# A mixture-of-experts block after cross attention: another order of routing, and low rank tables in one comparison

## The chip, the cores and the metric

The kernel runs on one core of a Trainium2 chip. The metric is the device time in microseconds of one execution.

## The reference, cut to what matters

`x` and a context are 4 batches of 256 tokens with 256 features. `x` is normalised, attends to the context with 16 heads of 16 features under a causal mask (keys and values are the context itself), and is added to the result. The sum is normalised again and goes through 16 experts, of which each token takes the best four:

```python
logits = x @ router_weight.T + router_bias
top_val, top_idx = jax.lax.top_k(logits, 4)
top_val = softmax(top_val)
gate_up = einsum('th,ehd->etd', x, gate_up_proj) + gate_up_proj_bias
glu = gate * sigmoid(gate * 1.702)          # gate and up clipped at 7
out = einsum('etd,edh->eth', (up + 1.0) * glu, down_proj) + down_proj_bias
x = x + (out * router_scores).sum(over experts)
```

## The kernel before, in words

The 1024 tokens are 8 tiles of 128, two per batch. There is no scheduler: each engine has one list of instructions in the order in which the code issues it, with semaphores between the engines. The list `steps` (built by `slot(b)`, once per batch) gives the order of the units of attention to all engines at once: "T" transposes queries and keys, "X" and "M" find row maxima, "S" is a pair of score matmuls (then the exponential on ScalarE and the causal select on POOL), "V" weighs the values, "O" turns a batch's output for VectorE. In the slot of the last batch the list also carries pieces of the routing of earlier batches: "Y" turns normalised tokens of a batch (TensorE), with a high part copied by ScalarE (`tokens_high`) and a low part by VectorE (`tokens_low`); "L" is the router's logits; "R" the ranks of each token among those of its expert. Routing goes by parts, not batches: part 0 is the first two batches (4 tiles), part 1 the third batch, part 2 the fourth (2 tiles each). `late` names the pieces that are issued by hand behind the list.

Per part, in this order:

- `router_logits` (TensorE, L1334, hi and lo part of the tokens, four matmuls a tile), then `router_logit` and `router_top` (VectorE, L966 to L993): logits, best four, their index, a one-hot `mask` of the experts chosen.
- `router_scores` (VectorE, L1003 to L1009): the softmax over the four, written beside the tokens into `y_ext`. The SyncE queue (SP) sends tokens and scores to DRAM, `y_rows(part)`, L467. `top_exp` on ScalarE gives it the exponential.
- `ranks` (TensorE, L1346, L1350) and `places` (VectorE, L1022 to L1033): from the mask a rank per (token, choice), split into the row inside a block of 128 (`low_f`) and a block number (`vblk_f`).
- For each of the 32 pairs of a tile and a choice two tables of 128 x 128 in f16: `low_hot` (`hot_lows`, VectorE, L1041, one tensor_scalar a pair) and `vblk_hot` (`hot_blocks`, POOL, L595, or `hot_highs`, VectorE, L1048). Part 0 has 16 pairs, parts 1 and 2 have 8 each.
- `slots` (TensorE, L1376): 32 matmuls over these pairs in one sum.

`counted` on POOL (L588) repeats the mask for `counts` (TensorE, L1360), from which `live_blocks`, `places` on TensorE (L1367) and `picks` find the 47 live blocks of tokens. `block_slots` (L1385, L1388) and `slot_tokens` (L1071 to L1075) give the token of each row. Then POOL gathers each block's tokens from DRAM by index (L646; the first six ahead of the loop, and only when all `y_rows` are in DRAM, which is `y_out`), and 47 expert blocks run: L1467 turns the tokens, L1489 is gate and up, L1508 down, L653 adds the rows back.

`rsqrt(b, which)` on POOL (L521) is the power instruction between a batch's variance and `tokens(b)` (VectorE, L849), which normalises it. For the last batch `attn_out`, `x1_rows`, `variance` (L892 to L845) stand ahead of it. `scores_t` (L1428) and `down_rows` (L1440) prepare the bias of the down projection; for parts 1 and 2 they stand behind `block_slots`, ahead of the first expert block.

Around the change VectorE, POOL, ScalarE and TensorE each have a tail written by hand behind the loop over `steps`.

## Time and profile before

| what | us |
|---|---|
| median of 3 runs | 312.12 (310.56 to 316.17) |
| profiled execution, own time | 311.56 |
| its span on the core | 309.8 |
| TensorE busy | 270.8 (87%) |
| POOL busy | 194.1 (63%) |
| VectorE busy | 182.3 (59%) |
| ScalarE busy | 122.8 (40%) |

The span runs from the first to the last instruction of the core; 1.76 us of the execution's own time lie outside it. Attention ends at about 103 us of the span, the expert blocks run from about 133 us to the end, and the routing lies between, partly inside attention's last slot. A busy share says little in that middle stretch: it is the waits that are to be read.

### The profile page before, as it was taken

To read this page: it belongs to the slowest core of one execution; us is meant where nothing else is said; L and a number is where in the kernel's file an instruction comes from. 1 tells how busy PE (TensorE), PEld (TensorE's weight loads), DVE (VectorE), ACT (ScalarE), POOL (GpSimd) and SP (SyncE) were. 2 spreads that over 40 slices of the span, in tenths; PEclk is the share of its full clock that TensorE was granted. 3 is DMA by queue.
4 is the path that set the end of the run, shared out by engine and by line. 5 is a ranking of instruction groups with operands and counts; after the bars stand their busy time and mean duration, and the time that the engine had idled before them with its cause. 6 is when DMAs were issued, how large, how long until landed. Compare 5 with 4: busy or idle time off the path is not lost.

```text
span 309.8 us, 5709 instructions
## 1 busy us (share of the span) xinstructions
PE 270.8 (87%) x1548; PEld 182.6 (59%) x1566; DVE 182.3 (59%) x505; ACT 122.8 (40%) x289; POOL 194.1 (63%) x239
## 2 busy tenths in 40 slices
PE   7787897897989743799998998999999999999895
PEld 7665475465565532555565665666566665656484
DVE  3997748957877978115444554455445466556433
ACT  3426555355464210143443443444434444434410
POOL 5983726524435889541876776877877877776400
PEclk9999998999997855569999999999999999999999
DMA  7706210100369872074554465445445545445464
GB/s 243 236 3 203 70 54 0 43 14 0 102 212 347 269 268 72 19 212 152 78 90 81 70 87 91 70 73 87 89 72 82 93 74 89 86 71 76 105 213 135
DMA packets 26877, 34.33 MB, mean 111 GB/s; under 512 B 2800, under 2 KB 21200, under 8 KB 26848
## 3 DMA queue, kind: packets, MB, share of 16 engines
q0 software_dynamic: 8592, 12.32, 24.6%
q1 hardware_dynamic: 17984, 21.39, 21.1%
q8 instruction: 15, 0.25, 0.3%
q10 hardware_dynamic: 272, 0.26, 0.2%
q14 instruction: 14, 0.11, 0.1%
HBM read 23.46 MB, written 10.43 MB: 109 GB/s over the span
## 4 chain that ended last, share of the span: by engine, by line
PE 62%; DVE 12%; POOL 9%; issue 6%; DMA 5%; ACT 2%; SPq 1%; another core or an unknown queue 1%; ACTq 0%; DVEq 0%
PE ps L1489 24%; PE ps L1508 10%; POOL vblk_hot L595 7%; DVE neg_max L872 6%; PE ps L1227 4%; PE ps L1522 3%; PE ps L1467 3%; DMA ctx_tok<-y_rows,slot_tok 3%; PE ps L1303 3%; PE ps L1498 3%; PE ps L1485 2%; PE ps L1246 2%; PE ps L1279 2%; DMA br_sb<-n_L_ffn_router_bias_dram 2%; PE ps L1440 1%
## 5 line engine op out<-in xcount | busy, mean ns | idle before, releaser
L1489 PE MATMUL ps<-w_all,q_norm 128*128 x188 | 89.6, 599 | 3.4 <-issue 1.9
L653 POOL DMA_INDIRECT acc_rows<-x_tok,slot_tok x44 | 70.0, 1591 | 32.6 <-ACT x_tok L808 27.2
L1151 DVE TENSOR_SCALAR v_aug<-ps 128x256 f32<-128x256 f32 x47 | 20.0, 425 | 72.3 <-PE ps L1489 46.2
L646 POOL DMA_INDIRECT ctx_tok<-y_rows,slot_tok x47 | 46.5, 989 | 16.7 <-issue 14.0
L1508 PEld LDWEIGHTS ps<-w_all,o_t 128*128 128x128 f32 x188 | 35.6, 190 | 25.7 <-issue 23.2
L792 ACT ACTIVATE v_aug<-v_aug 128x256 f32<-128x256 f32 x47 | 19.6, 417 | 76.9 <-DVE v_aug L1151 76.9
L1489 PEld LDWEIGHTS ps<-w_all,q_norm 128*128 128x128 f32 x188 | 35.2, 192 | 24.9 <-issue 23.2
L1508 PE MATMUL ps<-w_all,o_t 128*128 x188 | 48.3, 380 | 1.4 <-ACT o_t L797 1.4
L557 POOL TENSOR_SCALAR_AFFINE_SELECT w_all<-w_all 128x256 f32<-128x256 f32 (+1 forms) x48 | 23.3, 502 | 38.0 <-ACT w_all L706 37.1
L872 DVE TENSOR_REDUCE neg_max<-ps 128x2 f32<-128x512 f32 (+1 forms) x48 | 30.5, 684 | 7.4 <-PE ps L1252 5.1
L706 ACT ACTIVATE w_all<-ps 128x512 f32<-128x512 f32 x48 | 25.5, 601 | 23.3 <-PE ps L1279 23.1
L808 ACT ACTIVATE x_tok<-ps,ctx_tok 128x256 f32<-128x256 f32 x47 | 22.3, 474 | 19.8 <-PE ps L1508 18.9
L595 POOL TENSOR_SCALAR vblk_hot<-iota_h,vblk_f,tok_id 128x128 f16<-128x128 f16 x28 | 22.8, 826 | 2.3 <-DVE vblk_f L1031 2.3
L1162 DVE TENSOR_TENSOR v_aug<-v_aug 128x256 f32<-128x256 f32 x47 | 20.0, 426 | 7.1 <-ACT v_aug L792 5.5
L1169 DVE SCALAR_TENSOR_TENSOR o_t<-v_aug 128x256 f32<-128x256 f32 x47 | 20.0, 426 | 4.6 <-DVE v_aug L1162 0.4
L1467 PE MATMUL ps<-ident,ctx_tok 128*128 128x128 f32 x94 | 18.6, 282 | 1.4 <-DMA ctx_tok<-y_rows,slot_tok 1.3
L1156 DVE TENSOR_SCALAR v_aug<-ps 128x256 f32<-128x256 f32 x47 | 19.5, 415 | 0.0
L1246 PE MATMUL ps<-k_t,q_t 64*128 64x256 f32 (+1 forms) x128 | 13.6, 310 | 6.2 <-DVE neg_max L872 3.5
L786 ACT ACTIVATE q_norm<-ps 128x256 f32<-128x256 f32 x47 | 18.1, 384 | 0.3 <-PE ps L1467 0.3
L1498 PE MATMUL ps<-ident,o_t 128*128 128x128 f32 x94 | 18.0, 273 | 0.0
L1303 PE MATMUL ps<-w_all,v_aug 128*32 128x256 f32 x128 | 16.8, 409 | 1.0 <-ACT o_t L714 0.6
L797 ACT ACTIVATE o_t<-ps 128x256 f32<-128x256 f32 x47 | 17.6, 375 | 0.0
(155 smaller groups left out, 382.3 us busy)
## 6 DMA issues: line engine op xcount, KB each, us to landing
w_all<-_L_ffn_gate_up_proj_dram SPq DMA_DIRECT2D x16, 512.0 KB, 5.2
w_all<-in_L_ffn_down_proj_dram SPq DMA_DIRECT2D x16, 256.0 KB, 5.8
acc_rows<-x_tok SPq DMA_DIRECT2D x8, 256.0 KB, 9.1
x_tok<-in_x_dram SPq DMA_DIRECT2D x4, 256.0 KB, 4.4
y_ext<-acc_rows SPq DMA_DIRECT2D x4, 256.0 KB, 3.6
vblk_hot<-acc_rows SPq DMA_DIRECT2D x4, 256.0 KB, 3.7
out_dram<-y_ext SPq DMA_DIRECT2D x4, 256.0 KB, 2.2
ctx_tok<-in_ctx_dram SPq DMA_DIRECT2D x3, 256.0 KB, 5.1
```

The source lines that it names most:

```text
L557: pool.affine_select(out=blk, in_=blk, compare_op=ALU.is_ge, fill=0.0, base=0, pattern=[[0, n], [1, P]], channel_multiplier=-1).then_inc(s ...
L595: pool.tensor_scalar(vblk_hot[:, j, :], iota_h[:, :], vblk_f[:, j:j + 1], tok_id[:, j // TOP_K:j // TOP_K + 1], ALU.is_equal, ALU.mult).th ...
L646: pool.indirect_dma_start(out=xg[:, i % XG, :], out_offset=None, in_=y_dram[:, :], in_offset=bass.IndirectOffsetOnAxis(ap=slot_tok[:, i:i ...
L653: pool.indirect_dma_start(out=acc[i % 2][:, :], out_offset=bass.IndirectOffsetOnAxis(ap=slot_tok[:, i:i + 1], axis=0), in_=o_sb[:, i % 3, ...
L706: act.activation(prob[:, u % P_RING, :], ps[:, u % ST_RING, :], ACT.Exp, scale=SC).then_inc(exp_done, 1)
L808: act.activation(o_sb[:, i % 3, :], ps[:, 6 + i % 2, 0:D], ACT.Copy, scale=xg[:, i % XG, bass.ds(e + D, 1)]).then_inc(o_ready, 1)
L872: dve.tensor_reduce(neg_max[:, b % 2, t, p0 // 4, s, p0 % 4:p0 % 4 + np_], ps[:, work_bank(u), :].rearrange("p (a k) -> p a k", k=keys), A ...
L1303: pe.matmul(ps[rows, PVB, col:col + S], v_aug[:, b % 2, 0, h, :], p0, start=True, stop=True, skip_group_check=True)
L1467: tr = pe.transpose(ps[:, 2 + i % 2, k * P:(k + 1) * P], xg[:, i % XG, k * P:(k + 1) * P], ident[:, :])
L1489: mm = pe.matmul(o, x_t[:, i % 3, k, :], w_all[:, bass.ds(e, 1), k * 2 * F:(k + 1) * 2 * F].rearrange("p a n -> p (a n)"), start=False, st ...
L1498: tr = pe.transpose(ps[:, 4 + i % 2, f * P:(f + 1) * P], hid[:, i % 2, f * P:(f + 1) * P], ident[:, :])
L1508: mm = pe.matmul(o, hid_t[:, i % 2, f, :], w_all[:, bass.ds(e, 1), at:at + D].rearrange("p a n -> p (a n)"), start=(f == 0), stop=(f == FD ...
```

## The change

The third batch (part 1) gets its logits and ranks inside the last slot, where before only part 0 had them. In `slot`, for the last batch (Y, L and R take a batch or a part):

```diff
-                         ("V", b, (0,)), ("S", b, (5,)), ("V", b, (1, 2, 3)), ("R", 0, (0,)), ("V", b, (4,)),
-                         ("Y", 2, (0,)), ("V", b, (5, 6, 7)), ("O", b, (0, 1))]
+                         ("V", b, (0,)), ("Y", 2, (0,)), ("S", b, (5,)), ("V", b, (1, 2)), ("R", 0, (0,)),
+                         ("V", b, (3,)), ("L", 1, (0,)), ("V", b, (4, 5, 6, 7)), ("R", 1, (0,)), ("O", b, (0, 1))]
...
-        late = [("L", 1, 0), ("Y", B - 1, 0), ("R", 1, 0), ("L", 2, 0), ("R", 2, 0)]
+        late = [("Y", B - 1, 0), ("L", 2, 0), ("R", 2, 0)]
```

On POOL the power instruction of the third batch stands behind S1 of the last slot instead of S4, and the tables of part 1 are no longer POOL's:

```diff
-                    if n == 4 and b >= 1:
+                    if n == (1 if b == B - 1 else 4) and b >= 1:
                         rsqrt(b - 1, 1)
...
             counted(0)
-            hot_blocks(0, pairs_of(0)[:8])
+            hot_blocks(0, pairs_of(0)[:4])
+            counted(1)
+            hot_blocks(0, pairs_of(0)[4:8])
             rsqrt(B - 1, 1)
-            counted(1)
             hot_blocks(0, pairs_of(0)[8:])
-            hot_blocks(1, pairs_of(1))
             counted(2)
             hot_blocks(2, pairs_of(2)[:4])
```

On VectorE the low tables of a part are one comparison of two broadcast operands, and the order is another:

```diff
-                for j in pairs_of(part):
-                    ins = dve.tensor_scalar(low_hot[:, j, :], iota_h[:, :], low_f[:, j:j + 1], None, ALU.is_equal)
-                ins.then_inc(low_hot_ready, 1)
+                pairs = pairs_of(part)
+                n = len(pairs)
+                dve.tensor_tensor(low_hot[:, pairs.start:pairs.stop, :], iota_h[:, :].unsqueeze(1).to_broadcast([P, n, P]),
+                                  low_f[:, pairs.start:pairs.stop].unsqueeze(2).to_broadcast([P, n, P]), ALU.is_equal
+                                  ).then_inc(low_hot_ready, 1)
...
                 elif kind == "L":
                     router_logit(b)
+                    if b == 0:
+                        tokens(B - 2)
                     router_top(b)
-                    router_scores(b)
+                    if b == 1:
+                        router_scores(0)
                 elif kind == "R":
                     places(b)
-                    hot_lows(b)
-
-            router_logit(1)
+
+            router_scores(1)
             tokens(B - 1)
-            router_top(1)
+            hot_lows(0)
             tokens_low(B - 1)
-            places(1)
+            hot_highs(1, pairs_of(1))
+            hot_lows(1)
             router_logit(2)
             router_top(2)
-            router_scores(1)
-            router_scores(2)
             places(2)
-            hot_lows(1)
             hot_lows(2)
             hot_highs(2, pairs_of(2)[4:])
             live_blocks()
+            router_scores(2)
             picks()
```

On ScalarE `top_exp(1)` comes first behind the loop. On TensorE the tail is:

```diff
-            router_logits(1)
             scores_t(0)
             down_rows(0)
+            tokens_t(B - 1)
             down_rows(1)
-            tokens_t(B - 1)
-            ranks(1)
             router_logits(2)
-            slots(0)
             ranks(2)
             counts()
+            slots(0)
+            slots(1)
             places()
-            slots(1)
             slots(2)
```

Beside this, `neg_half` becomes a view of a tile `small` that also holds a constant 1.0 which nothing reads, a view `low_dist` is named and not used, and `low_f` has a semaphore of its own (`low_ready`) in place of a settle.

The first place is VectorE, from the places of part 0 to the logits of the last batch. In the kernel before (`idx8`, `onehot`, `mask`: best four, one-hot, mask; `picked`, `low_f`: the ranks; `w_all<-iota_h,low_f`: low tables):

```order
L1033 CAST low_f<-low_i 128x16
L1041 TENSOR_SCALAR w_all<-iota_h,low_f 128x128 x16
L912 TENSOR_TENSOR y_lo<-ps,y_hi 128x2x256
L892 RECIPROCAL r_den<-ps 128x16 x2
L895 TENSOR_TENSOR attn<-ps,r_den 128x256 x2
L904 TENSOR_TENSOR x_tok<-x_tok,attn 128x256 x2
L836 BN_STATS stats<-x_tok 128x6 x2
L842 BN_AGGR mv<-stats 128x2 x2
L845 TENSOR_SCALAR var_eps<-mv 128x2
L966 TENSOR_TENSOR logits<-ps,br_sb 128x32
L969 TENSOR_TENSOR logits<-ps,logits 128x32
L973 MAX top8<-logits 128x8 x2
```

And in the changed kernel, behind the variance of the last batch:

```order
L850 TENSOR_SCALAR var_eps<-mv 128x2
L1008 TENSOR_TENSOR logit_d<-logit_e,mask 128x32
L1010 TENSOR_REDUCE top_s<-logit_d 128x2
L1012 RECIPROCAL top_r<-top_s 128x2
L1014 TENSOR_TENSOR y_ext<-logit_d,top_r 128x2x16
L854 TENSOR_SCALAR y_ext<-x_tok,mv,rstd 128x256 x2
L1047 TENSOR_TENSOR w_all<-iota_h,low_f 128x2048
L917 TENSOR_TENSOR y_lo<-ps,y_hi 128x2x256
L1055 TENSOR_SCALAR vblk_hot<-iota_h,vblk_f,tok_id 128x128 x8
L1047 TENSOR_TENSOR w_all<-iota_h,low_f 128x1024
L971 TENSOR_TENSOR logits<-ps,br_sb 128x32
L974 TENSOR_TENSOR logits<-ps,logits 128x32
```

The low tables of part 0 have moved from ahead of attention's last output to behind it, and part 1's tables stand where its logits stood.

The second place is POOL behind the last slot. Before (`mask_rep`: `counted`; `rstd`: the power instruction; `vblk_hot`: `hot_blocks`):

```order
L557 AFFINE_SELECT w_all<-w_all 128x512 x2
L588 COPY mask_rep<-mask 128x512
L595 TENSOR_SCALAR vblk_hot<-iota_h,vblk_f,tok_id 128x128 x8
L521 TENSOR_TENSOR rstd<-var_eps,neg_half 128x2
L588 COPY mask_rep<-mask 128x256
L595 TENSOR_SCALAR vblk_hot<-iota_h,vblk_f,tok_id 128x128 x16
L588 COPY mask_rep<-mask 128x256
L595 TENSOR_SCALAR vblk_hot<-iota_h,vblk_f,tok_id 128x128 x4
```

And now:

```order
L561 AFFINE_SELECT w_all<-w_all 128x512 x2
L593 COPY mask_rep<-mask 128x512
L600 TENSOR_SCALAR vblk_hot<-iota_h,vblk_f,tok_id 128x128 x4
L593 COPY mask_rep<-mask 128x256
L600 TENSOR_SCALAR vblk_hot<-iota_h,vblk_f,tok_id 128x128 x4
L525 TENSOR_TENSOR rstd<-var_eps,small 128x2
L600 TENSOR_SCALAR vblk_hot<-iota_h,vblk_f,tok_id 128x128 x8
L593 COPY mask_rep<-mask 128x256
L600 TENSOR_SCALAR vblk_hot<-iota_h,vblk_f,tok_id 128x128 x4
```

Eight tables are gone from the list, all of them ahead of the last four, and the COPY of part 1 stands among the first eight.

## Rows read from the trace of the kernel before

**Rows 1.** The page, the chain that ended last: shares of the span by engine, by line.
```profile
PE 62%; DVE 12%; POOL 9%; issue 6%; DMA 5%; ACT 2%; SPq 1%; another core or an unknown queue 1%; ACTq 0%; DVEq 0%
PE ps L1489 24%; PE ps L1508 10%; POOL vblk_hot L595 7%; DVE neg_max L872 6%; PE ps L1227 4%; PE ps L1522 3%; PE ps L1467 3%; DMA ctx_tok<-y_rows,slot_tok 3%; PE ps L1303 3%; PE ps L1498 3%; PE ps L1485 2%; PE ps L1246 2%; PE ps L1279 2%; DMA br_sb<-n_L_ffn_router_bias_dram 2%; PE ps L1440 1%
```

**Rows 2.** The chain in order of time, 80 to 140 us: start, us, what.
```profile
100.61 6.05 POOL vblk_hot L595 x7
...
109.92 9.83 POOL vblk_hot L595 x13
...
122.88 3.25 POOL vblk_hot L595 x4
...
126.18 1.05 PE ps L1376 x8
```

**Rows 3.** The timeline of the last slot: start, us, engine, line, what [idle before].
```profile
93.85 1.11 PE L1279 MATMUL ps<-q_t,k_t 64*128 64x128 f32 x8
...
94.27 0.68 POOL L521 TENSOR_TENSOR rstd<-var_eps,neg_half 128x2 f32<-128x2 f32 x1
...
99.75 3.00 DVE L1041 TENSOR_SCALAR w_all<-iota_h,low_f 128x128 f16<-128x128 f16 x16
...
101.58 1.07 PE L1314 MATMUL ps<-ident,o_t 128*128 128x128 f32 x8 [0.78 <-ACT o_t L714]
...
103.27 0.35 DVE L892 RECIPROCAL r_den<-ps 128x16 f32<-128x16 f32 x2
```

**Rows 4.** VectorE's groups, shapes kept apart: count | busy us, mean ns.
```profile
L1162 DVE TENSOR_TENSOR v_aug<-v_aug 128x256 f32<-128x256 f32 x47 | 20.0, 426 | 7.1 <-ACT v_aug L792 5.5
...
L1048 DVE TENSOR_SCALAR vblk_hot<-iota_h,vblk_f,tok_id 128x128 f16<-128x128 f16 x4 | 1.1, 339 | 0.0
...
L989 DVE TENSOR_TENSOR onehot<-iota_c,idx_f 128x256 f32<-128x256 f32 x1 | 0.5, 511 | 0.0
```

**Rows 5.** The timeline of VectorE behind the last slot.
```profile
112.97 0.19 DVE L966 TENSOR_TENSOR logits<-ps,br_sb 128x32 f32<-128x32 f32 x1 [0.68 <-PE ps L1334]
...
115.18 0.37 DVE L993 TENSOR_REDUCE mask<-onehot 128x32 bf16<-128x128 f32 x1
115.46 0.21 DVE L1003 TENSOR_TENSOR logit_d<-logit_e,mask 128x32 f32<-128x32 f32 x1
...
116.38 0.27 DVE L1003 TENSOR_TENSOR logit_d<-logit_e,mask 128x32 f32<-128x32 f32 x1
...
118.36 0.29 DVE L1022 TENSOR_TENSOR picked<-onehot,ps 128x128 f32<-128x128 f32 x1 [0.94 <-PE ps L1350]
...
119.66 3.46 DVE L1041 TENSOR_SCALAR w_all<-iota_h,low_f 128x128 f16<-128x128 f16 x16
123.05 1.12 DVE L1048 TENSOR_SCALAR vblk_hot<-iota_h,vblk_f,tok_id 128x128 f16<-128x128 f16 x4
...
128.33 0.21 DVE L1073 SCALAR_TENSOR_TENSOR slot_tok<-ps,pad_f 128x48 uint32<-128x48 f32 x1
```

**Rows 6.** POOL's L595 in 99 to 107, then in 109 to 127: min/median/max ns.
```profile
L595 POOL TENSOR_SCALAR vblk_hot<-iota_h,vblk_f,tok_id x8: 785/842/1052, 99.7 to 105.9; 128x128 f16<-128x128 f16 x8
L595 POOL TENSOR_SCALAR vblk_hot<-iota_h,vblk_f,tok_id x20: 784/794/908, 109.9 to 125.3; 128x128 f16<-128x128 f16 x20
```

**Rows 7.** Busy us (x instructions) by microsecond: PE, PEld, DVE, ACT, POOL; PEclk, DMA.
```profile
91.00:92.00 1.00, 0.13 (x2) 0.13 (x4) 0.92 (x7) 1.00 (x3) 0.61 (x2) 1.00 1.05 366
...
93.00:94.00 1.00, 1.00 (x10) 0.40 (x6) 0.93 (x5) 0.78 (x2) 0.90 (x3) 0.50 1.03 343
...
105.00:106.00 1.00, 0.34 (x2) 0.31 (x3) 0.97 (x3) 0.59 (x1) 1.00 (x2) 1.00 1.02 320
...
120.00:121.00 1.00, 0.00 (x0) 0.00 (x0) 1.00 (x7) 0.00 (x0) 1.00 (x3) 0.50 0.00 0
```

**Rows 8.** DMA issues: what, issuing queue, count, KB each, median us to landing.
```profile
acc_rows<-x_tok SPq DMA_DIRECT2D x8, 256.0 KB, 9.1
...
y_rows<-y_ext SPq DMA_DIRECT2D x2, 272.0 KB, 2.2
```

More of the change, by code:

```diff
@@ L113, in xattn_moe @@
         mv = sb("mv", [P, NT, 2])
-        neg_half = sb("neg_half", [P, TB])
+        small = sb("small", [P, TB + 1])
+        neg_half = small[:, 0:TB]
+        one_f = small[:, TB:TB + 1]
         var_eps = sb("var_eps", [P, 2, NT])
@@ L152, in xattn_moe @@
         vblk_hot = sb("vblk_hot", [P, NT * TOP_K, P], F16)
+        low_dist = mask_diag.rearrange("p a n -> p (a n)").bitcast(F16).rearrange("p (a n) -> p a n", n=P)
         live_b = sb("live_b", [P, 1], BF16)
@@ L233, in xattn_moe @@
         vblk_hot_ready = sem("vblk_hot_ready")
+        low_ready = sem("low_ready")
         low_hot_ready = sem("low_hot_ready")
@@ L568, in ffn_tables @@
                 pool.memset(ones_b[:, :], 1.0).then_inc(ffn_consts, 1)
+                pool.memset(one_f[:, :], 1.0).then_inc(ffn_consts, 1)
                 step(pool.memset(before_b[:, :], 0.0))
@@ L767, in b_rows @@
                                ACT.Copy).then_inc(b_rows_ready, 1)
+            top_exp(1)
             scores_turned(0)
@@ L772, in _ @@
             b_rows(1)
-            top_exp(1)
             top_exp(2)
@@ L924, in block_tables @@
             def block_tables():
-                dve.wait_ge(ffn_consts, 5)
+                dve.wait_ge(ffn_consts, 6)
                 step(dve.tensor_copy(iota_h[:, :], iota_c[:, :]))
@@ L940, in bias_high @@
                 dve.wait_ge(bias_in, 48)
-                dve.wait_ge(ffn_consts, 7)
+                dve.wait_ge(ffn_consts, 8)
                 step(dve.tensor_copy(bias_1[:, :], raw_b[:, :]))
@@ L1032, in places @@
                                          high_i[:, tk], ALU.mult, ALU.add).then_inc(vblk_ready, 1)
-                step(dve.tensor_copy(low_f[:, tk], low_i[:, tk]))
+                dve.tensor_copy(low_f[:, tk], low_i[:, tk]).then_inc(low_ready, 1)
             def hot_lows(part):
-                settle()
+                dve.wait_ge(low_ready, part + 1)
                 if part == 0:
                     dve.wait_ge(work_full, slot_of[("T", B - 1, 7)] + 1)
-                for j in pairs_of(part):
-                    ins = dve.tensor_scalar(low_hot[:, j, :], iota_h[:, :], low_f[:, j:j + 1], None, ALU.is_equal)
-                ins.then_inc(low_hot_ready, 1)
+                pairs = pairs_of(part)
[3 more added lines that the diff above has]
+                                  ).then_inc(low_hot_ready, 1)
             def hot_highs(part, pairs):
@@ L1118, in _ @@
                         queries(b + 2)
-                    if n == 5 and b >= 1:
+                    if n == 5 and 1 <= b < B - 1:
                         tokens(b - 1)
@@ L1344, in ranks @@
                 if part == 0:
-                    pe.wait_ge(ffn_consts, 6)
+                    pe.wait_ge(ffn_consts, 7)
                 mm = pe.matmul(ps[:, bank, 0:(hi - lo) * E], before_b[:, :], mask[:, lo:hi, :].rearrange("p t e -> p (t e)"),
```

## The prediction, on record before the changed kernel ran

> **What bounds the kernel now.** I read the chain of waits first, by line and then in order of time, and after it the timeline of the stretch in which it leaves TensorE. Over the whole span 62% of the chain is TensorE, most of it the expert blocks at L1489 and L1508, and 7% is one POOL line, L595 [rows 1]. In order of time that 7% is one piece of the program: after attention's last slot POOL builds `vblk_hot`, a table per pair of a token tile and a choice, and the three pieces shown hold 24 of its 28 instructions and end at 126.13; then come slot matmuls, slot numbers and down rows, and the first expert block [rows 2]. The reader should see that behind 126.18 everything hangs on the last of POOL's 28 instructions. The expert stretch that follows is not touched by the change. So the question is: when does POOL finish its last four tables, when does VectorE give it the block numbers for them, and does something else come last afterwards?
>
> Why POOL is late: an L595 instruction takes 0.785 when alone, up to 1.05 when VectorE works beside it [rows 6]. Sixteen of them, for batches 1 and 2, run from 109.9 to 122.5, and only then come the four of batch 3. VectorE had their block numbers ready at about 119.6, where its own low tables begin [rows 5]: POOL was 3.2 us behind VectorE.
>
> **The change, step by step.** Times are those of the profiled execution (span 309.8, own time 311.56; the median of the runs shown is 312.12, 0.56 above it).
>
> *Start of the slot.* The power instruction (0.68, [rows 3]) now stands ahead of the selects of S2 on POOL. Its input is there at about 91.2, where the selects began at 91.4, so they start near 91.9: +0.5 for V0 behind them. Then the four transposes of Y2 stand ahead of S5. Eight such take 1.07 at full clock [rows 3]; the granted clock there is half [rows 7], so four cost about 1.1. S5 comes at about 95.2, not 93.85. Behind it the slot also takes batch 2's logits (8 small matmuls, 0.9) and ranks (0.3), and loses Y2 and the wait for VectorE ahead of it. The ranks need the mask of batch 2, and O(3) is queued behind them: mask and o_t both come near 102, so that wait is hidden with nothing to spare. I put O(3) at 102.6, +1.0 against 101.58 [rows 3].
>
> *VectorE ahead of O(3).* Out go 16 low tables (3.00, [rows 3]). In come logits and mask of batch 2 (2.6, by the same work for batch 3, 112.97 to 115.55), its places (1.3, 118.36 to 119.66), and the first scores, which moved behind them at no change (all [rows 5]). `attn_out` starts at about 104.1 against 103.3: +0.8, of which 0.4 is O(3) itself. This is the price of the move, and the next steps have to earn it back.
>
> *The broadcast comparison.* No row of before shows a 2048-element form. The nearest rows are two-input VectorE instructions on 256 elements, 0.426 at L1162 and 0.511 with the same broadcast at L989 [rows 4]. With a cycle per element at 0.96 elements per ns, 256 elements are 0.27 and the rest, 0.16, is fixed: 2048 elements are 2.3, 1024 are 1.2. The lower bound is half of the element part (1.2 and 0.7), the upper the L989 row scaled by elements (4.1 and 2.0). I take 2.3 and 1.2, by L1162, which has 47 instances. Against 3.00 for the 16 separate ones and 3.46 for the last 16, part 0 saves 0.7 and the two parts of eight save 1.0 together.
>
> *VectorE between O(3) and the logits of batch 3.* The path before is attention's output, statistics, power on POOL, tokens, logits. Gone from between are logits, mask and places of batch 2, about 3.6. Added are one part's scores (0.92, 115.46 to 116.38, [rows 5]; partly beside POOL's 0.7), low tables of part 0 (2.3), eight `hot_highs` of batch 2 (8 x 0.28 = 2.2: four stand 0.28 apart, 1.12 in all, the 339 of [rows 4] overlaps), and low tables of part 1 (1.2). The logits of batch 3 are taken up at 115.1 against 112.97: +2.2. So VectorE is made later here; what pays is behind it.
>
> *Behind the mask of batch 3.* Mask at 115.1 + 2.6 = 117.7. Before it was ready at 115.55 but its ranks stood on TensorE behind slots(0), which waited for POOL, so `picked` ran at 118.36. Now ranks come first and `picked` runs at about 118.2. Places end at 119.5. One part's low table (1.2) replaces two (3.46), so VectorE's low and high tables end at 121.8 and not 124.0; `live` 0.4, scores of batch 3 0.9 (they moved behind it) and `pick` 0.5 end at 123.6, against 125.2.
>
> *POOL.* 20 tables where 28 were. The 8 that go are 6.3 us. The 8 of batch 1 run from about 107.9, after the power instruction, to 114.2; POOL then idles some 3.4 until the mask of batch 3, which is slack. Its last four start at 119.5, not 122.86, and take 3.14 to 3.26, or 0.3 more beside VectorE (0.865 against 0.785 each is what the first eight showed, [rows 2, 6]). They end at 122.9 to 123.0, against 126.13: -3.1. Since `pick` (123.6) is earlier than the end of the last slots (124.1), slot numbers come at 125.4 against 128.54 [rows 5]. Everything behind keeps its order, so the end moves by 3.1 as well.
>
> *Gathers.* They also need the last `y_rows` transfer, issued when the scores of batch 3 are there: 116.5 before, about 123.2 now. It lands 2.2 later [rows 8], at 125.4, just as the slot numbers. Hidden, without cover.
>
> *Clock.* TensorE is granted half speed (1.2 of 2.4 GHz) in 93 to 97 and again from 107 to 137 [rows 7]; its gaps at 91 and 105, each ahead of a fall, stay, so I count no change. The other edits (a constant column more, an unused view, a semaphore in place of a settle, SP's `y_rows(0)` and the weight loads behind it some 2 to 5 us later, first needed by the seventh expert block) I put at 0 to 0.1 each; cover gone, they would show as a gather waiting.
>
> Sum: 311.56 - 3.1 = 308.5.
>
> **A rule that speaks against it.** POOL's L595 took up to 1.05 beside VectorE's tables, against 0.785 alone [rows 6]: 0.3, never the whole of another instruction. The Trainium skill (SBUF — State Buffer, "Who interferes with whom") says that a VectorE instruction with two SBUF inputs and a GpSimd instruction that reads SBUF exclude each other for a whole instruction. The broadcast comparison has two SBUF inputs and is long, which no row of before has beside L595. By that rule the sum would be near 311.
>
> The skill (VectorE: DVE Perf Modes, "The perf-mode tier table") also gives two-input instructions twice the rate when all is 16-bit. Here `low_f` is 32-bit, so by it the plain rate holds, as I took it.
>
> **Rivals.**
> 1. *Broadcast blocks POOL.* For: POOL does slow beside VectorE. Against: by a tenth on the mean of the first eight. Price: the comparison (1.2) and four highs (1.1) stand beside POOL's last four, 2.3; and 5.7 (2.3 + 1.2 + 2.2) beside the eight of batch 1, which would end at 119.9, their COPY at 120.3, 0.8 past the 119.5. Together 3.1, less the 0.3 already counted: 308.5 + 2.8 = 311.3.
> 2. *Comparison at double rate.* The f16 output speaks for it, the f32 operand with no step against it. 1.1 + 0.5 come off ahead of the logits of batch 3, and places end 1.6 earlier: 308.5 - 1.6 = 306.9.
> 3. *The last y_rows transfer takes the place of the wait.* It is issued 6.7 later and the gathers wait for it. Two of 272 KB landed in 2.2, but `x_tok` writes of the same size queued behind weight loads took 9.1 in the median [rows 8], and the weights now start later. Landed at 123.2 + 9.1 = 132.3 the first gather goes 3.5 later than its 128.84: 315.1, slower than before. It decides from a landing above 5.6; against it is that the DMA engines are idle from 120 on.
>
> **Numbers.** Forecast 0.62, rival 1 0.18, rival 2 0.12, rival 3 0.08. The forecast's own range is 307.3 to 309.9 (the slot 1 longer or shorter). The whole range is 306.2 to 311.4: it takes in rivals 1 and 2, and leaves out rival 3 and some of the edges. A measurement of this kernel can tell about 2%, 6.2 us. Faster by more needs double the gain: 0.05. Slower by more needs rival 3 and the slot together: 0.03. Within 2%: 0.92.
>
> **What would show it.** POOL idle for about 3 ahead of the last COPY into `mask_rep`; L595 x20; the broadcast at 2.3 and 1.2; `picked` of batch 3 near 118.2; slot numbers near 125.4; the first gather right behind them. The forecast is wrong if O(3) comes later than 103.5, if L595 stretches beyond 1.1, or if the first gather starts over 0.5 behind the slot numbers.

## The result, and the profile after

| what | before | changed |
|---|---|---|
| median of 20 runs, us | 313.76 (310.56 to 319.02) | 311.67 (307.07 to 315.38) |
| ratio, 95% interval | | 0.9891 (0.9855 to 0.9926) |
| profiled execution, own time | 311.56 | 307.52 |
| its span | 309.8 | 305.8 |
| mean granted TensorE clock | 0.939 | 0.950 |

The ratio leaves disturbed runs out, among them ten of the changed kernel's 20; the medians of all 20 and 20, as in the table, stand at 0.9933. By the ratio the change takes off 1.1%, or 3.4 of 311.56 us, inside the band that was called no change. The changed kernel was compared with the one before three times in all (twice more in experiments 8 and 12), with ratios of 0.9891, 0.9899 and 0.9988. The third interval, 0.9945 to 1.0030, does not overlap the first: the gain is not the same in every comparison. What goes with that is in the table of the experiments and behind experiment 12.

Batches are counted here as the first to the fourth or last. The prediction counts them from 0, so its batch 3 is the last one and its batch 2 the third.

The page of the changed kernel, the chain that ended last, to be held against [rows 1]:

```profile
PE 67%; DVE 16%; DMA 5%; issue 5%; POOL 3%; ACT 1%; SPq 1%; ACTq 0%; POOLq 0%; DVEq 0%
```

POOL's share has gone from 9% to 3%, VectorE's from 12% to 16%. The same chain in order of time, from the tokens of the last batch on (start, us, what), answers to [rows 2]:

```profile
109.94 2.19 DVE w_all L1047
112.13 0.60 DVE y_lo L917
112.73 1.84 DVE vblk_hot L1055 x8
114.57 1.13 DVE w_all L1047
115.70 0.11 DVE logits L971
...
118.48 0.30 DVE picked L1027
...
119.67 4.28 POOL vblk_hot L600 x4
...
124.00 0.64 PE ps L1384 x8
...
126.64 3.71 PE ps L1448 x8
```

Before, the chain ran along POOL's tables from 109.9 on. Now it runs along VectorE's list, and POOL has only the last four tables in it. The reader should see the two broadcast comparisons (L1047) and the eight tables of the third batch (L1055) on it: they are on the path, as the prediction had them. The timeline of POOL:

```profile
103.76 3.65 POOL L600 TENSOR_SCALAR vblk_hot<-iota_h,vblk_f,tok_id 128x128 f16<-128x128 f16 x4
108.27 0.72 POOL L525 TENSOR_TENSOR rstd<-var_eps,small 128x2 f32<-128x2 f32 x1 [0.85 <-DVE var_eps L850]
108.99 9.83 POOL L600 TENSOR_SCALAR vblk_hot<-iota_h,vblk_f,tok_id 128x128 f16<-128x128 f16 x8
118.77 0.39 POOL L593 COPY mask_rep<-mask 128x256 bf16<-128x256 bf16 x1
119.67 4.27 POOL L600 TENSOR_SCALAR vblk_hot<-iota_h,vblk_f,tok_id 128x128 f16<-128x128 f16 x4 [0.52 <-DVE vblk_f L1036]
126.13 1.25 POOL L651 DMA_INDIRECT ctx_tok<-y_rows,slot_tok  x1 [2.19 <-DVE slot_tok L1080]
```

The eight tables were to take 6.3 and to leave POOL idle for 3.4. They took 9.83, nothing idle is left ahead of the COPY, and the last four took 4.27 instead of 3.3. Single tables in that stretch show why:

```profile
109.78 2.94 POOL L600 TENSOR_SCALAR vblk_hot<-iota_h,vblk_f,tok_id 128x128 f16<-128x128 f16 x1
...
114.48 1.89 POOL L600 TENSOR_SCALAR vblk_hot<-iota_h,vblk_f,tok_id 128x128 f16<-128x128 f16 x1
...
116.36 0.80 POOL L600 TENSOR_SCALAR vblk_hot<-iota_h,vblk_f,tok_id 128x128 f16<-128x128 f16 x1
```

And VectorE beside them (compare [rows 4] and [rows 5]):

```profile
109.86 2.27 DVE L1047 TENSOR_TENSOR w_all<-iota_h,low_f 128x2048 f16<-128x2048 f16 x1
...
114.49 1.21 DVE L1047 TENSOR_TENSOR w_all<-iota_h,low_f 128x1024 f16<-128x1024 f16 x1
115.63 0.18 DVE L971 TENSOR_TENSOR logits<-ps,br_sb 128x32 f32<-128x32 f32 x1
...
118.48 0.29 DVE L1027 TENSOR_TENSOR picked<-onehot,ps 128x128 f32<-128x128 f32 x1 [0.54 <-PE ps L1358]
...
119.69 1.24 DVE L1047 TENSOR_TENSOR w_all<-iota_h,low_f 128x1024 f16<-128x1024 f16 x1
120.85 1.02 DVE L1055 TENSOR_SCALAR vblk_hot<-iota_h,vblk_f,tok_id 128x128 f16<-128x128 f16 x4
...
123.05 0.31 DVE L1072 TENSOR_SCALAR pick<-iota_c,row,live_f 128x48 fp32r<-128x48 f32 x1
...
125.61 0.21 DVE L1080 SCALAR_TENSOR_TENSOR slot_tok<-ps,pad_f 128x48 uint32<-128x48 f32 x1
```

A table takes 0.80 alone. The one that meets the 2.27 comparison takes 2.94, the one that meets the 1.21 takes 1.89: less than 0.15 short of the table and the whole comparison together. It goes one way only: in all eleven profiles with such comparisons VectorE's instruction takes 2.27 to 2.31 or 1.21 to 1.24, close to the 2.3 and 1.2 that were forecast from instructions of another form, and a table of POOL that began up to 0.2 before or after it is the one held.

Then TensorE, from attention's last output (L1322) by the last slot matmuls (L1384) and down rows (L1448) to the first expert transposes (L1473):

```profile
103.26 1.06 PE L1322 MATMUL ps<-ident,o_t 128*128 128x128 f32 x8
...
124.00 0.62 PE L1384 MATMUL ps<-w_all,vblk_hot 128*128 128x128 f16 x8 [1.57 <-POOL vblk_hot L600]
...
126.57 3.78 PE L1448 MATMUL ps<-b_down,score_t 16*128 16x256 f32 x8
130.28 1.12 PE L1473 MATMUL ps<-ident,ctx_tok 128*128 128x128 f32 x4
```

The first gather came 2.71 earlier (128.84 before), the first expert transposes 2.91 earlier (133.19 before). Of the span's 4.0 the expert stretch gave the other 1.1: 176.61 before, 175.52 now. Nothing was changed there, and in the changed kernel's two other profiles it was 176.13 and 175.61; in experiment 5, which keeps the order of before, it was 175.88. So that 1.1 is put down to scatter.

### The profile page after: what moved, and what is told of

Its sections match the earlier page's. It is cut to its first block, busy times and chain, and to the rows that moved or that the text cites. A ratio compares the mean times of both kernels' runs of the same rounds, so it can differ in the third digit from the quotient of the medians.

```text
span 305.8 us, 5699 instructions
## 1 busy us (share of the span) xinstructions
PE 271.9 (89%) x1566; PEld 180.8 (59%) x1566; DVE 181.6 (59%) x484; ACT 122.8 (40%) x289; POOL 192.6 (63%) x232
## 4 chain that ended last, share of the span: by engine, by line
PE 67%; DVE 16%; DMA 5%; issue 5%; POOL 3%; ACT 1%; SPq 1%; ACTq 0%; POOLq 0%; DVEq 0%
PE ps L1495 24%; PE ps L1514 11%; DVE neg_max L877 6%; PE ps L1491 4%; PE ps L1311 4%; PE ps L1473 4%; PE ps L1235 3%; PE ps L1528 3%; PE ps L1504 3%; PE ps L1254 3%; DMA ctx_tok<-y_rows,slot_tok 2%; DMA br_sb<-n_L_ffn_router_bias_dram 2%; PE ps L1260 2%; PE ps L1287 2%; DVE x_tok L909 1%
## 5 line engine op out<-in xcount | busy, mean ns | idle before, releaser
L813 ACT ACTIVATE x_tok<-ps,ctx_tok 128x256 f32<-128x256 f32 x47 | 22.3, 475 | 19.8 <-PE ps L1514 19.5
L600 POOL TENSOR_SCALAR vblk_hot<-iota_h,vblk_f,tok_id 128x128 f16<-128x128 f16 x20 | 20.9, 1056 | 1.2 <-DVE vblk_f L1036 1.2
L1491 PE MATMUL ps<-bias_w,sel_e 128*128 128x512 bf16 x47 | 18.2, 388 | 2.4 <-issue 2.2
L1473 PE MATMUL ps<-ident,ctx_tok 128*128 128x128 f32 x94 | 18.8, 285 | 0.3 <-DMA ctx_tok<-y_rows,slot_tok 0.2
L791 ACT ACTIVATE q_norm<-ps 128x256 f32<-128x256 f32 x47 | 18.1, 385 | 0.1
```

Source lines behind the costliest of these rows:

```text
L813: act.activation(o_sb[:, i % 3, :], ps[:, 6 + i % 2, 0:D], ACT.Copy, scale=xg[:, i % XG, bass.ds(e + D, 1)]).then_inc(o_ready, 1)
L1473: tr = pe.transpose(ps[:, 2 + i % 2, k * P:(k + 1) * P], xg[:, i % XG, k * P:(k + 1) * P], ident[:, :])
L1491: pe.matmul(o, sel_e[:, bass.ds(e, 1)].to_broadcast([P, P]), bias_w[:, :], start=True, stop=False)
```

## Experiments

To compare profiles whose attention took different times, times are counted from the start of `r_den` of the last batch (103.27 before, 105.01 changed), the first VectorE instruction behind attention's last output. "Slot" is the time to it from `r_den` of the third batch (87.94 before, 88.24 changed). All in us. "Slot numbers" is the end of `slot_tok`, "experts" the start of the first expert transposes, and "clock" the granted TensorE clock at the last eight slot matmuls, which follow POOL's last table: 18.1 to 19.0 behind `r_den` in most kernels, 22.9 to 26.7 in the kernel before and in experiments 2, 4 and 5.

| kernel | slot | picked | slot numbers | gather | experts | clock |
|---|---|---|---|---|---|---|
| before | 15.33 | 15.09 | 25.27 | 25.57 | 29.92 | 0.50 |
| changed | 16.77 | 13.47 | 20.81 | 21.12 | 25.27 | 1.00 |
| 1 all tables separate | 18.10 | 14.40 | 21.36 | 22.46 | 26.02 | 0.50 |
| 2 broadcast in before | 15.09 | 17.18 | 29.07 | 29.37 | 33.72 | 0.50 |
| 3 last part separate | 16.74 | 13.46 | 19.89 | 21.51 | 24.78 | 1.00 |
| 4 part 1 behind slot | 15.67 | 19.26 | 26.60 | 26.90 | 31.05 | 1.00 |
| 5 offload in before | 15.56 | 15.04 | 25.35 | 25.66 | 30.00 | 0.50 |
| 6 with 3, scores early | 18.09 | 13.99 | 20.95 | 21.26 | 25.60 | 0.50 |
| 7 scores behind picks | 16.75 | 13.46 | 20.78 | 21.84 | 25.23 | 1.00 |
| 8 changed again | 16.80 | 13.47 | 20.81 | 21.12 | 25.27 | 1.00 |
| 9 down rows early | 17.43 | 13.45 | 21.32 | 21.63 | 24.90 | 0.50 |
| 10 with 6 and 9 | 16.77 | 13.79 | 20.23 | 20.54 | 23.80 | 1.00 |
| 11 the same again | 18.10 | 14.01 | 20.98 | 21.28 | 24.49 | 0.50 |
| 12 changed, beside 11 | 17.37 | 13.46 | 21.36 | 21.67 | 26.01 | 0.50 |

The slot and the clock go together in the ten profiles with part 1's routing in the slot. In the five with a slot of 16.74 to 16.80 the granted clock fell to 0.50 at 3.3 to 3.6 into the slot, was back 6.8 later, and stood at 1.00 at the slot matmuls. In the two with 17.37 and 17.43 it fell at 4.8 to 5.0, and in the three with 18.09 and 18.10 it stayed at 0.50 for 13.7; in these five it stood at 0.50 at the slot matmuls. The changed kernel itself shows the first pattern twice and the second once. So a difference between two rows counts as the edit's only where their clocks agree, and the slot only where the patterns agree.

**1. All low tables as separate instructions, in the changed order.**

```diff
-                dve.tensor_tensor(low_hot[...], iota_h broadcast, low_f broadcast, ALU.is_equal).then_inc(low_hot_ready, 1)
+                for j in pairs_of(part):
+                    ins = dve.tensor_scalar(low_hot[:, j, :], iota_h[:, :], low_f[:, j:j + 1], None, ALU.is_equal)
+                ins.then_inc(low_hot_ready, 1)
```

> The changed kernel with the low tables built one by one again (32 tensor_scalar), all else as changed. Theory (a two-input broadcast shuts POOL out for its whole length: single L600 of 2.94, 1.89 and 1.89 us in the changed kernel where 0.79 is usual): POOL's eight tables of the tail take 6.3 to 7.0 us instead of 9.83 and its last four 3.1 to 3.3 instead of 4.27; VectorE loses 0.7 + 0.4 + 0.4 us, so picked of batch 3 comes about 1.2 later, and slot numbers at 125.8 to 126.1 against 125.82: no change in time, within 0.3%. Rival (the broadcast is what pays, POOL is slow beside VectorE whatever it runs): L600 keeps the stretched rows and slot numbers come 1.5 later or more.

Ratio 0.9951 (0.9902 to 1.0001). POOL's two pieces of tables:

```profile
113.00 6.99 POOL L600 TENSOR_SCALAR vblk_hot<-iota_h,vblk_f,tok_id 128x128 f16<-128x128 f16 x8
122.75 0.40 POOL L593 COPY mask_rep<-mask 128x256 bf16<-128x256 bf16 x1 [2.76 <-DVE mask L998]
124.42 3.36 POOL L600 TENSOR_SCALAR vblk_hot<-iota_h,vblk_f,tok_id 128x128 f16<-128x128 f16 x4 [1.27 <-DVE vblk_f L1036]
131.29 1.25 POOL L651 DMA_INDIRECT ctx_tok<-y_rows,slot_tok  x1 [3.51 <-DMA y_rows<-y_ext]
```

9.83 became 6.99, 4.27 became 3.36, and the idle ahead of the COPY is there (2.76): the comparison is what held POOL. The tables cost VectorE 2.90, 1.44 and 1.59 in place of 2.27, 1.21 and 1.24, so everything behind `r_den` came 0.9 later to POOL's last four, which then took 0.9 less. Against experiment 12, with the clock at the same level, slot numbers (21.36 and 21.36) and experts (26.02 and 26.01) agree, one profile each; the first gather, which waits for the last transfer here, is 0.8 later at no cost. **The broadcast comparison is worth nothing in this kernel**; what it saves on VectorE it takes from POOL.

**2. The broadcast comparison alone, in the kernel before** (the first edit turned round).

> The kernel before with nothing but the broadcast comparison. There POOL is the bound from 99.7 to 126.1. Theory (POOL shut out for the length of the comparison): POOL's tables take 2.2 us more in the first piece and 2.3 more in the second, slot numbers at 132 to 133 instead of 128.5, the time 3.5 to 4.5 us (1.1 to 1.4%) above the kernel before. Rival (they share, POOL is slowed by some 10% beside VectorE): slot numbers at 128.0, time equal to the kernel before within 0.5 us.

Ratio 1.0122 (1.0050 to 1.0195), slower. The timeline of POOL:

```profile
101.82 8.60 POOL L595 TENSOR_SCALAR vblk_hot<-iota_h,vblk_f,tok_id 128x128 f16<-128x128 f16 x8 [2.28 <-DVE vblk_f L1031]
...
113.66 14.43 POOL L595 TENSOR_SCALAR vblk_hot<-iota_h,vblk_f,tok_id 128x128 f16<-128x128 f16 x16
...
128.42 3.11 POOL L595 TENSOR_SCALAR vblk_hot<-iota_h,vblk_f,tok_id 128x128 f16<-128x128 f16 x4
```

Where POOL bounds, the comparisons (2.31, then 1.22 and 1.22) cost most of their length: 8.60 against 6.92 and 14.43 against 12.63, 3.5 of the 3.8 by which slot numbers came later. The two tables that met them took 2.92 and 2.79. Slot numbers stood at 133.94 of this span, a little behind the theory's 132 to 133.

**3. Separate tables for the last part alone.**

```diff
+                if part == len(PARTS) - 1:
+                    for j in pairs_of(part):
+                        ins = dve.tensor_scalar(low_hot[:, j, :], iota_h[:, :], low_f[:, j:j + 1], None, ALU.is_equal)
+                    ins.then_inc(low_hot_ready, 1)
+                    return
```

> The changed kernel with the low tables of the last part alone built one by one, so that no two-input instruction stands beside POOL's last four tables. Theory: first of the four L600 0.8 to 0.9 instead of 1.89, the four end at about 122.9 instead of 123.94, VectorE 0.4 later, slot numbers at 124.8 instead of 125.82: 1.0 us faster than the changed kernel, 4.5 below the kernel before. Rival (VectorE's path through live, scores and pick is as late): slot numbers 125.2 or later, under 0.6 gained.

Ratio 1.0019 (0.9974 to 1.0065). Slot numbers came 0.92 earlier, as the theory says (POOL held for the whole comparison), but the 1.0 us in time that it forecast did not follow. The first gather:

```profile
129.06 1.25 POOL L651 DMA_INDIRECT ctx_tok<-y_rows,slot_tok  x1 [3.50 <-DMA y_rows<-y_ext]
```

It now waits for the transfer of the last tokens and scores, and starts 1.62 behind the slot numbers instead of 0.31. The scores of the last batch end at 18.35 and the gather starts at 21.51: 3.16. In experiments 1 and 7 the same difference is 3.17 and 3.16. In the changed kernel the scores end at 17.93, so this transfer would allow a gather at 21.1, and it starts at 21.12: the two waits end together there. The experts still came 0.49 earlier than in the changed kernel, but this run's ratio shows no gain at all. Its profile lost 2.6 ahead of O2, where TensorE's clock was at 0.50 from 60 to 66 us and that of the changed kernel at 1.00.

**4. Logits and ranks of part 1 behind attention's last output, still ahead of the loop's end.**

```diff
-                         ("V", b, (3,)), ("L", 1, (0,)), ("V", b, (4, 5, 6, 7)), ("R", 1, (0,)), ("O", b, (0, 1))]
+                         ("V", b, (3, 4, 5, 6, 7)), ("O", b, (0, 1)), ("L", 1, (0,)), ("R", 1, (0,))]
```

> The changed kernel with logits and ranks of the third batch behind attention's last output instead of inside the slot; tables, splits and tails as changed. Theory (the slot hides about 5 us of VectorE's serial work in the waits of attention): slot numbers at 130 to 131, 4.5 to 5 us later than in the changed kernel, the time 1 to 2 us above the kernel before. Rival (the gain is only that POOL has eight tables less): slot numbers within 1 us of 125.8, time within 0.3% of the changed kernel.

Ratio 1.0192 (1.0114 to 1.0270). The slot is 1.10 shorter than in the changed kernel's first profile (1.70 shorter than in experiment 12), and slot numbers come 5.79 later at the same clock, later even than before the change. The change's gain hangs on this one placement: for 1.1 to 1.7 us in the slot the part's routing leaves the path behind attention. The ratio says 6 us, more than the forecast 1 to 2 and more than the routing explains (experts 1.13 later than before the change); it rests on three runs, and the rest is not explained. The placement alone, with part 1's tables still on POOL and TensorE's tail in the old order, was not run.

**5. Part 1's block tables moved from POOL to VectorE, in the kernel before.**

```diff
-            hot_blocks(1, pairs_of(1))
...
+            hot_highs(1, pairs_of(1))
```

> The kernel before, with the eight block tables of the third batch taken from POOL and built by VectorE behind the places of the fourth batch; nothing else. Theory (VectorE is only 2 us behind POOL, so POOL's 6.3 us come off and VectorE's queue, longer by 2.1, ends last): slot numbers 1.5 to 2 us later than in the kernel before (27.1 after the start of attention's last output, against 25.3), time 0 to 0.8% above it. Rival (POOL alone was the bound, eight tables less are 6 us less): slot numbers 3 us or more earlier, ratio 0.99 or less.

Ratio 1.0044 (0.9999 to 1.0089), no gain. VectorE's end of the routing, where it now issues all tables at the end:

```profile
122.35 1.87 DVE L1047 TENSOR_SCALAR vblk_hot<-iota_h,vblk_f,tok_id 128x128 f16<-128x128 f16 x8
124.14 2.89 DVE L1040 TENSOR_SCALAR w_all<-iota_h,low_f 128x128 f16<-128x128 f16 x16
126.95 0.97 DVE L1047 TENSOR_SCALAR vblk_hot<-iota_h,vblk_f,tok_id 128x128 f16<-128x128 f16 x4
128.71 0.31 DVE L1064 TENSOR_SCALAR pick<-iota_c,row,live_f 128x48 fp32r<-128x48 f32 x1
```

The forecast of 1.5 to 2 us later was too much: slot numbers moved by 0.08, and the rival's 3 us earlier did not come either. POOL is done at 126.07 of that span and then idle for 5.82, but `pick` is ready only at 129.0 (22.8 behind `r_den`, 21.90 before). The wait went from POOL to VectorE. Relieving POOL pays only if VectorE's work for the third batch is out of the way as well, which is what moving its logits into the slot does.

**6. Experiment 3 with the scores of the last batch ahead of its places.**

```diff
+            router_scores(2)
             places(2)
...
-            router_scores(2)
             picks()
```

> The changed kernel with the last part's low tables one by one and the scores of the fourth batch ahead of its places, so that the last y_rows transfer leaves some 4 us earlier. Theory (the first gather waits for the later of slot numbers and scores + 3.2 us; in the run with only the last tables separate it was the second, 1.6 us behind the slot numbers): the gather starts 0.3 us behind the slot numbers, at 20.5 after the start of attention's last output against 21.1 in the changed kernel, 0.6 us (0.2%) faster. Rival (slot numbers bind in any case and places are late now): 21.1 or later.

Ratio 0.9866 (0.9786 to 0.9946). Scores end at 14.07, and the gather is back at 0.31 behind the slot numbers: it no longer waits for the transfer. But it starts at 21.26 and not at the forecast 20.5, which is the number that the rival named: `picked` is 0.5 later behind the scores, and the clock is at 0.50. At that level the experts are 0.41 earlier than the changed kernel's (experiment 12). The ratio rests on three runs and can't show so little.

**7. The changed kernel with those scores behind `picks`.**

> The changed kernel with the scores of the fourth batch behind pick instead of ahead of it. Theory (scores + 3.2 us): slot numbers unchanged at 20.8, the first gather at 22.3, waiting on the DMA of y_rows and 1.5 behind the slot numbers; 1.1 us (0.4%) slower than the changed kernel. Rival (the transfer of 272 KB is done in 2.2 and hidden): gather at 21.1 as before.

Ratio 0.9969 (0.9927 to 1.0012). The gather starts 0.72 later (21.84; 22.3 was forecast) and waits for the transfer, but the experts start at 25.23, where they started before, so the path shows none of the 1.1 us that this was to cost. The ratio, 0.7% above that of experiment 8 with overlapping intervals, can't settle it. TensorE was in its down rows (L1448) until then. So in the changed kernel the gather has some 0.8 of cover, and the last down rows stand on the path.

**8. The changed kernel again.**

> The changed kernel once more, beside the others of this call. Ratio to the kernel before 0.985 to 0.993; from the start of attention's last output on VectorE (the reciprocals of the fourth batch) the slot numbers end 20.8 us later and the first gather starts 21.1 later, as in its first profile. If the 1.1% measured at first was chance, the ratio is above 0.995.

Ratio 0.9899 (0.9845 to 0.9954), as forecast, with the same times in every column of the table within 0.03.

**9. The turned scores and down rows of part 1 ahead of the ranks of part 2, while TensorE waits for the mask** (ScalarE's copies of both moved to the same place).

```diff
+            scores_t(1)
+            down_rows(2)
             ranks(2)
...
-            scores_t(1)
             scores_t(2)
-            down_rows(2)
```

> The changed kernel with TensorE's turn of the scores and down rows of batch 3 (scores_t(1), down_rows(2)), and ScalarE's copies of them, moved ahead of the ranks and places sums of part 2. Theory (in the changed kernel the first expert transposes wait for TensorE's down rows behind the sum for the slot numbers, not for the gather): with these 2.8 us done while TensorE waits for the mask, the first expert transposes start 3.3 us behind the gather, at 24.4 us behind the reciprocal of batch 4's attention instead of 25.3; slot numbers stay at 20.8. Ratio to the kernel before about 0.986, where the changed kernel has 0.989. Rival: down rows end behind the mask (13.0), so ranks, picked and all behind them come later by up to 1 us, slot numbers at 21.5 or more, and nothing is gained.

Ratio 0.9958 (0.9910 to 1.0006). Experts start 3.27 behind the gather, as expected, now waiting for it:

```profile
131.80 0.66 PE L1473 MATMUL ps<-ident,ctx_tok 128*128 128x128 f32 x2 [1.17 <-DMA ctx_tok<-y_rows,slot_tok]
```

`picked` was not delayed (13.45), so the rival is wrong; yet slot numbers came at 21.32 and not 20.81. That difference is the clock, as experiment 12 then showed: at its level the changed kernel has 21.36 and 26.01, so this edit alone brings the experts 1.11 forward. It does not bring them to the forecast 24.4, as the clock was at 0.50. The ratio can't tell the gain from nothing.

**10. Experiments 6 and 9 together.**

> The same move of the down rows, with the last part's low rank tables made one by one and the scores of batch 3 multiplied ahead of the places of part 2 (the last two experiments' edits together). Theory: slot numbers at 20 to 20.9, gather 0.3 behind them, first expert transposes 3.3 us behind the gather, 23.7 to 24.5 where the changed kernel has 25.3; ratio about 0.984. Rival: the places of part 2 wait for the scores' multiplication, slot numbers at 21 or later as in that experiment, and the transposes no earlier than 24.6.

Ratio 0.9879 (0.9770 to 0.9988). Slot numbers 20.23, gather 20.54, experts 23.80, each where the theory had it. The ratio rests on two runs.

**11 and 12. The combined kernel again, and the changed kernel beside it on the same chip.**

> The last experiment's kernel once more, beside the changed kernel on the same chip. Theory (the profile of the last run, where slot numbers were ready at 20.2 and the first expert transposes began at 23.8 us behind the reciprocal of batch 4's attention, 1.5 earlier than in the changed kernel, holds again): 20.2 and 23.8 within 0.3, and a time 1.5 us or 0.5% under the changed kernel's. Rival: what is gained ahead of the expert blocks goes into a lower TensorE clock or a longer tail, and the two times agree within 0.2%.

> The changed kernel itself, beside the combined one: slot numbers at 20.8, gather at 21.1, first expert transposes at 25.3 us behind that reciprocal, ratio to the kernel before 0.989 by both theories.

Ratios 0.9879 (0.9825 to 0.9933) and 0.9988 (0.9945 to 1.0030). Both profiles missed what was expected of them: the combined kernel's slot numbers came at 20.98 and its experts at 24.49, not within 0.3 of 20.2 and 23.8, and the changed kernel's at 21.36 and 26.01, not 20.8 and 25.3. The ratios put the combined kernel 1.1% ahead of the changed one, more than its 1.5 us explain; but the four and eight runs that they rest on have means of 309.22 and 310.92, which is 1.7 us. The changed kernel itself differed from its two other profiles in its clock. Busy time by microsecond (PE, PEld, DVE, ACT, POOL, clock, DMA) in the changed kernel's first profile, while POOL ends its tables:

```profile
122.00:123.00 1.00, 0.35 (x3) 0.10 (x1) 0.87 (x6) 0.00 (x0) 1.00 (x2) 0.83 0.00 0
123.00:124.00 1.00, 0.00 (x1) 0.01 (x1) 0.32 (x2) 0.00 (x0) 0.94 (x2) 1.00 0.08 28
124.00:125.00 1.00, 0.71 (x10) 0.61 (x10) 0.00 (x0) 0.28 (x1) 0.00 (x0) 1.00 0.71 250
```

And in experiment 12, with what TensorE did then:

```profile
122.00:123.00 1.00, 0.60 (x5) 0.26 (x3) 0.90 (x6) 0.00 (x0) 1.00 (x2) 0.50 0.00 0
123.00:124.00 1.00, 0.00 (x0) 0.00 (x0) 0.57 (x4) 0.00 (x0) 1.00 (x2) 0.50 0.00 0
124.00:125.00 1.00, 0.72 (x8) 0.72 (x8) 0.00 (x0) 0.00 (x0) 0.23 (x1) 0.50 0.78 276
```

```profile
124.28 1.03 PE L1384 MATMUL ps<-w_all,vblk_hot 128*128 128x128 f16 x8 [1.57 <-POOL vblk_hot L600]
...
131.29 1.12 PE L1473 MATMUL ps<-ident,ctx_tok 128*128 128x128 f32 x4
```

The slot matmuls take 0.62 at full clock (2.4 GHz) and 1.03 at half (1.2 GHz), and with those behind them slot numbers come 0.55 and experts 0.74 later, of the same kernel. Its slot was 0.60 longer too, with the clock's fall 1.6 later in it. At equal clock the combined kernel gains 25.27 − 23.80 = 1.47 at full, and 26.01 − 24.49 = 1.52 at half. **That gain of 1.5 us, 0.5%, is shown at both levels.** That the combined kernel is faster in time than the changed one is supported by this one comparison of few runs; against the first ratio of 0.9891 there is no difference.

The record has the mean clock of every run, and over the changed kernel's 38 runs the time goes with it: the three at 0.950 took 307.1 to 307.8, the eight at 0.939 took 308.5 to 311.5, the six at 0.923 took 311.8 to 314.0. The ratio of 0.9891 rests on ten runs at 0.934 to 0.950, the one of 0.9988 on eight at 0.923 to 0.939. What makes one execution take the one pattern and the next another is open.

## Why the prediction was right, and where it was not

The forecast was 308.5 for the profiled execution, a gain of 3.1. Measured were 307.52, and 308.2 by the ratio (0.9891 × 311.56). The mechanism forecast is in the main the one that happened: POOL's tables of part 1 left the path, VectorE's list took their place, and the first expert transposes came 2.91 earlier, against 3.1. But that agreement is in part luck, a sum of misses that cancel:

- *Start of the slot and O(3).* Forecast 102.6, measured 103.26; the ranks of part 1 waited 1.00 for the mask, which I had called hidden. `r_den` was to come 0.8 later and came 1.74 later, as it also stands behind the places (`low_f` ends at 105.09). This term was undersized by 0.9, of which 0.3 lay ahead of the slot already (88.24 against 87.94). Experiment 4 gives the price of part 1's logits and ranks in the slot: 1.10 against this profile, 1.70 against experiment 12.
- *The broadcast comparison.* 2.3 and 1.2 forecast, 2.27 and 1.21 to 1.24 measured. Its duration was right; rival 2, the double rate, is out.
- *VectorE to `picked`.* Forecast 118.2, measured 118.48. This is 13.5 behind `r_den`, where the steps gave 14.1: the eight `hot_highs` took 1.92, not 2.2, and the rest gave a little each. So of the miss of 0.9 in the slot 0.3 was left. The step had not shown all its working: the terms that it lists add up to some 3.8 for the logits of the last batch, not 2.2. Most of the difference is two waits of VectorE ahead of those logits, 0.77 and 0.68 in the trace of before, which are gone in the changed one and which it did not name.
- *POOL.* The last four were to "take 3.14 to 3.26, or 0.3 more beside VectorE": this step failed. They took 4.27 (and the prediction had named a table of over 1.1 as what would make it wrong; three took 1.9 to 2.9), as the comparison held the first of them for nearly its whole length. POOL's end came at 123.94, not 122.9 to 123.0. For the same reason the idle time of 3.4 ahead of the COPY was not there.
- *Behind POOL.* The end of `slot_tok` was 2.4 behind POOL's last table before, and 1.9 in the changed kernel, by the clock that rose to full. I had said "I count no change" for the clock; it gave back 0.55 here and 0.2 in the down rows, in this profile, and nothing in that of experiment 12. With that clock the experts would have come only 2.2 earlier.
- *The expert stretch.* Counted at nothing; it came 1.1 shorter, which the other profiles show to be scatter.

*Rival 1* deserved more than its 0.18 as a mechanism and less as a price. The table of 1.05 that spoke against it [rows 6] stood beside VectorE instructions with one tensor input in SBUF, and bears on another case. The trace of before did hold the right case in short form, `onehot` with two inputs in SBUF, with POOL idle and then beside a table:

```profile
108.77 0.29 DVE L989 TENSOR_TENSOR onehot<-iota_c,idx_f 128x128 f32<-128x128 f32 x1
...
114.64 0.51 DVE L989 TENSOR_TENSOR onehot<-iota_c,idx_f 128x128 f32<-128x128 f32 x1
```

There VectorE's instruction was the longer for it and the table (0.79) was not, so the engines do meet, but the row doesn't tell who waits when VectorE's is long. The rule of the Trainium skill (SBUF — State Buffer, "Who interferes with whom"), that a VectorE instruction with two SBUF inputs and a reading GpSimd instruction exclude each other whole, agrees with 2.94 for 0.80 and 2.27. That POOL holds VectorE for a whole instruction, no run here shows. The price of 2.8 was too high for two reasons the traces show: the 3.5 that the comparisons cost the eight tables all fell on POOL's idle time, and VectorE's four separate tables hardly count: POOL's last four took 0.79 to 0.82 each behind the first, and in experiment 3, with eight more of them beside, 3.36 in all. What is left is 1.0, and experiment 3 shows it: 0.92.

*Rival 3*, the last transfer of tokens as the new wait, did not decide in the changed kernel, but stood right beside the path. Its "landing above 5.6" is where the kernel would have become slower than before; by the prediction's own times the gather would wait from 2.5 on. I had 2.2 for the transfer, from issue to landing [rows 8]; from the end of the scores to the gather it is 3.16. The margin was not "hidden, without cover" but the down rows on TensorE, 0.8 (experiment 7).

What the range rested on, the terms of the middle stretch, held. What I had left out of it was the difference between comparisons of one kernel: 0.9891 and 0.9988 differ by 3 us, as much as the whole gain. The runs behind the second are at lower mean clocks, and the profiles show 0.60 of it in the slot and 0.74 behind it; the rest was not located.

## What to carry to other kernels

Before an instruction on VectorE is made one long two-input instruction, look at what POOL does beside it, and compare short two-input instructions of the trace at hand with and without POOL beside them. Whether it costs anything depends on POOL's slack there. When a late engine is relieved, list what ends next, and next after that: here POOL, VectorE's `pick`, the last transfer and TensorE's down rows each stood within about 1 us of being the one that is waited for, so one edit soon met the next wait: separate tables gave 0.5 of their 0.9, the down rows moved ahead gave 1.1, and the three edits together 1.5. Before a difference of 1 us between two profiles is put down to an edit, compare their granted clocks over the whole stretch. Work whose inputs are there early belongs where its engine waits, as the third batch's logits in the slot and the down rows ahead of the ranks.

## What the runs showed of the hardware

- A long VectorE instruction with two SBUF inputs stops a POOL instruction that reads SBUF for nearly its whole length: 0.80 became 2.94 beside 2.27, and 1.89 beside 1.21 or 1.24. VectorE's took 2.27 to 2.31 and 1.21 to 1.24 in all eleven profiles.
- A short one can be held itself: `onehot`, 128x128, took 0.29 with POOL idle and 0.51 beside a table of 0.79 (kernel before; the same 0.51 and 0.79 in experiment 9).
- VectorE's 16-bit table instructions with one tensor input slow POOL's tables only in part: 0.90 and 0.91 beside the eight of the third batch (changed kernel), 0.80 to 1.05 in experiment 1, where such tables stood beside most of the eight (6.99 for what takes 6.3 alone).
- TensorE's granted clock took either level in the same stretch of the same program (0.50 in experiment 12, up to 1.00 in two other profiles), around the same instructions, at the same distance from `r_den`. It changed the routing's end by 0.74, while the slot ahead of it was 0.60 longer.
- Where the first expert transposes wait for the first gather, they start 3.2 to 3.3 behind its issue on POOL (3.27, 3.27, 3.26 and 3.21 in experiments 3, 9, 10 and 11).
